# Recommendation tower on one core: ten embedding tables by one-hot matmul, taken two at a time, and features laid out by pairs of samples

## The reference

```python
e = jnp.stack([tbl_0[ids[:, 0]], ..., tbl_25[ids[:, 25]]], axis=1)
combined = jnp.concatenate([dense_features[:, None, :], sparse_features], axis=1)   # 512 x 27 x 128
interactions = jnp.einsum('bfd,bgd->bfg', combined, combined)
interactions_flat = interactions[:, iu, ju]                                         # 351 pairs
h = jnp.concatenate([dense, interactions_flat, dense], axis=1)                      # 607
h = jnp.maximum(h @ W_top1 + b_top1, 0.0)     # 512
h = jnp.maximum(h @ W_top2 + b_top2, 0.0)     # 256
y = h @ W_top3                                # 1
```

## Time and profile before

| what | us |
|---|---|
| median of 3 runs | 112.77 (111.9 to 113.47) |
| span of the profiled execution | 110.6 |
| PE busy | 98.0 (89%) |
| DVE busy | 87.3 (79%) |
| ACT busy | 85.4 (77%) |
| POOL busy | 67.7 (61%) |
| stage one on PE, first to last one-hot matmul | 7.92 to 60.3 |
| stage two on PE | 60.9 to 108.7 |

### The profile page before, as it was taken

How to read it: one execution, slowest core, us unless ns; L and a number is a source line. 1 busy time by engine, 2 the same in 40 slices (tenths; PEclk the granted TensorE clock), 3 DMA queues, 4 the chain that set the end, 5 groups by cost and what they waited for, 6 DMA issues and landing times. The chain is left out here.

```text
span 110.6 us, 2569 instructions
## 1 busy us (share of the span) xinstructions
PE 98.0 (89%) x931; PEld 77.7 (70%) x931; DVE 87.3 (79%) x216; ACT 85.4 (77%) x180; POOL 67.7 (61%) x68
## 2 busy tenths in 40 slices
PE   4967989949999999999999976999999977987991
PEld 2334846538788877768667965899899876975960
DVE  4469989689999999988989899945992849999001
ACT  4369697999999999999971899966796679683310
POOL 3577777777777777788888977777777700000000
PEclk9999999999999999999999999999999999999999
DMA  4889989944987789999110123212222210000000
GB/s 75 278 294 362 357 246 390 330 169 76 281 172 261 289 170 381 413 378 310 56 27 25 42 68 77 65 49 61 67 70 54 74 25 0 6 0 0 0 0 1
DMA packets 7868, 16.59 MB, mean 150 GB/s; under 512 B 2156, under 2 KB 3568, under 8 KB 7600
## 3 DMA queue, kind: packets, MB, share of 16 engines
q1 hardware_dynamic: 5648, 11.84, 31.9%
q0 software_dynamic: 1920, 3.94, 12.6%
q10 hardware_dynamic: 288, 0.66, 2.2%
HBM read 16.43 MB, written 0.00 MB: 148 GB/s over the span
## 5 line engine op out<-in xcount | busy, mean ns | idle before, releaser
L329 POOL DMA_INDIRECT rows<-in_gathered_tables,row_at x60 | 66.8, 1114 | 20.1 <-issue 17.7
L695 PE MATMUL gram_ps<-one_hot,table_hi 128*128 128x512 f32 x94 | 38.8, 413 | 4.3 <-DVE one_hot L512 2.5
L697 PE MATMUL gram_ps<-one_hot,table_lo 128*128 128x512 f32 x94 | 37.0, 394 | 0.0
L512 DVE TENSOR_SCALAR one_hot<-hot_ids_sb,row_ids 128x512 fp32r<-128x512 int32 x83 | 35.4, 480 | 1.9 <-DMA hot_ids_sb<-in_hot_ids 1.9
L540 DVE COPY pairs<-gram_ps 27x128 f32<-27x128 f32 (+3 forms) x76 | 25.3, 333 | 6.0 <-PE gram_ps L633 4.9
L695 PEld LDWEIGHTS gram_ps<-one_hot,table_hi 128*128 128x128 f32 x94 | 17.6, 188 | 13.3 <-DVE one_hot L512 5.4
L435 ACT COPY pairs<-gram_ps 27x128 f32<-27x128 f32 (+3 forms) x68 | 22.7, 334 | 3.9 <-PE gram_ps L633 3.1
L697 PEld LDWEIGHTS gram_ps<-one_hot,table_lo 128*128 128x128 f32 x94 | 17.7, 189 | 2.5
L633 PE MATMUL gram_ps<-features_t 128*59 128x56 f32 x512 | 15.9, 219 | 1.9 <-ACT features_t L344 1.3
L633 PEld LDWEIGHTS gram_ps<-features_t 128*59 128x59 f32 x512 | 14.7, 134 | 3.6 <-ACT features_t L344 1.7
L400 ACT COPY features_t<-gram_ps 128x512 f32<-128x512 f32 (+2 forms) x12 | 12.3, 1040 | 4.9 <-PE gram_ps L697 4.9
(11 more groups left out here) (45 smaller groups left out, 58.1 us busy)
## 6 DMA issues: line engine op xcount, KB each, us to landing
table_sb<-in_hot_tables SPq DMA_DIRECT2D x10, 512.0 KB, 5.6
hot_ids_sb<-in_hot_ids SPq DMA_DIRECT2D x11, 256.0 KB, 4.8
w_pairs_sb<-in_w_pairs SPq DMA_DIRECT2D x1, 1024.0 KB, 8.6
w_again_sb<-in_w_again SPq DMA_DIRECT2D x1, 1024.0 KB, 11.2
rows<-in_gathered_tables,row_at POOLq DMA_INDIRECT x60, 4.9
table_sb<-in_hot_tables ACTq DMA_DIRECT2D x1, 512.0 KB, 5.2
w_sb<-in_w SPq DMA_DIRECT2D x1, 512.0 KB
table_sb<-in_hot_tables SPq DMA_DIRECT2D x2, 128.0 KB, 5.3
```

The source lines that it names most:

```text
L329: pool.indirect_dma_start(rows[:, p % rows_ring, m, :], None, gathered_tables, bass.IndirectOffsetOnAxis(ap=row_at[:, t, at:at + 1], axis= ...
L512: nc.vector.tensor_scalar(one_hot_at(i), hot_ids_sb[:, of % ids_ring, :], row_id(n, c), None, ALU.is_equal).then_inc(one_hot_dve, 1)
L695: nc.tensor.matmul(hot_bank(of), table_hi[:, n % 3, own], one_hot_at(i), start=(begins and c == 0), stop=False)
L697: last = nc.tensor.matmul(hot_bank(of), table_lo[:, n % 3, own], one_hot_at(i), start=False, stop=(ends and c == count - 1))
```

## The change

- Table 0 (10 parts) is gathered, not multiplied: ten hot tables with 84 parts, sixteen gathered with 64 indirect DMAs (16 per tile; a tile's first pass has four, the others three). `rows` holds 7 passes, not 9.
- The hot tables run in groups of two (`HOT_GROUPS`; the first and last group have one table). One DVE instruction makes the one-hot rows of both tables (128x1024, L509 of the changed kernel); ACT makes none. The split in high and low goes by pieces of four parts, with two PSUM banks in turn, not three.
- `features_t` is laid out by pairs of samples: two samples' numbers for one slot are neighbours, so a copy of one table writes 8 bytes in every 256. The products' operands are read with a step of two numbers; they have 64 and 54 columns (before 59 and 56). The transposes write PSUM without a step. The samples are reordered on input, so that the copies into `pairs` write neighbouring numbers.
- The two sets of dense weights are loaded compactly (128x1024), added by one instruction, and moved to their places in `w_pairs_sb` by 14 DMAs on SP, ahead of the ten DMAs that join the dense features.
- The zeroing of `pairs` and of half of the free slots goes to POOL, ahead of the gathers. Two warm-up matmuls, not four.

```diff
-HOT = (0, 2, 3, 1, 7, 13, 16, 19, 21, 23, 25)
-HOT_PARTS = (10, 10, 10, 8, 8, 8, 8, 8, 8, 8, 8)
+HOT_GROUPS = ((1,), (2, 3), (7, 13), (16, 19), (21, 23), (25,))
+GROUP_PARTS = (8, 10, 8, 8, 8, 8)
+PIECE_PARTS = 4
...
-TURN_EARLY = {5 + p: p for p in range(9)}
-WARM = (4, 4, 4, 2)
+TURN_BEHIND = {(1, 4): 0, (1, 9): 1, (2, 3): 2, (2, 7): 3, (3, 3): 4, (3, 7): 5, (4, 3): 6, (4, 7): 7, (5, 7): 8}
+WARM = (4, 4)
...
-    table_ring, ids_ring, rows_ring = 5, 5, 9
+    piece_ring, ids_ring, rows_ring, hot_ring = 8, 3, 7, 8
...
-        features_t = sbuf("features_t", [P, batch, SLOTS])
+        features_t = sbuf("features_t", [P, batch // 2, SLOTS, 2])
...
# SP, after the loads of the weights
+                sp.wait_ge(w_summed, 1)
+                sp.wait_ge(pair_weights_in, 16)
+                for d, (p, i) in enumerate(dense_places()[:dim]):
...
+                        sp.dma_start(w_pairs_sb[p:p + run, i, :], w_dense_sb[d:d + run, 0, :]).then_inc(w_joined, 16)
+                sp.wait_ge(pairs_zeroed, 1)
                 join_dense(0)
                 join_dense(1)
...
# ACT, stage one
+                for g in range(n_groups):
+                    if g >= 1:
+                        place_hot(g - 1)
...
+                    for q in ahead[:2]:
+                        split_piece(q)
+                    for p in turns[:-1]:
+                        place_pass(p)
+                    for q in ahead[2:]:
+                        split_piece(q)
...
+                    for p in turns[-1:]:
+                        place_pass(p)
...
# DVE, stage one
+                        if 1 <= g < n_groups - 1:
+                            behind = (5, 6, 8, 9) if g == 1 else (1, 3, 5, 7)
+                            if c in behind and behind.index(c) < len(pieces_of(g + 1)):
+                                low_part(pieces_of(g + 1)[behind.index(c)])
+                        if g == n_groups - 1 and c == 3:
+                            sum_dense_weights()
...
# PE, products
-                            last = nc.tensor.matmul(gram_ps[64 * h:64 * h + SLOTS + FEATURES, n % 2, q, 0:4 * COLUMNS],
-                                                    flat_features[:, b * SLOTS:b * SLOTS + SLOTS + FEATURES],
-                                                    features_t[:, b:b + 2, 0:2 * COLUMNS], start=True, stop=True)
+                            last = nc.tensor.matmul(gram_ps[64 * h:64 * h + 2 * SLOTS, n % 2, q, 0:2 * FEATURES],
+                                                    features_t[:, two:two + 2, :, h].rearrange("p a s -> p (a s)"),
+                                                    features_t[:, two:two + 2, 0:FEATURES, h], start=True, stop=True)
...
-                pe.wait_ge(w_summed, PAIR_PARTS)
+                pe.wait_ge(w_joined, 16 * n_w_runs)
                 layer1(0, (0, 1, 2, 3))
```

More of the change, by code:

```diff
@@ L58, in pair_places @@
                     yield 32 * k + g, i, None, False
-FREE_ROWS = ((27, 5, 0, 4), (59, 5, 0, 4), (91, 5, 0, 3), (123, 3, 0, 3), (64, 64, 3, 1))
+FREE_ROWS = ((27, 5, 0, 4), (59, 5, 0, 4), (91, 5, 0, 3), (64, 64, 3, 1), (123, 5, 0, 3))
 def dense_places():
-    return [(p, i) for row, rows, part, parts in FREE_ROWS for p in range(row, row + rows) for i in range(part, part + parts)]
+    return [(p, i) for row, rows, part, parts in FREE_ROWS for i in range(part, part + parts) for p in range(row, row + rows)]
 def pieces():
@@ L76, with sample_order @@
 PIECES = pieces()
+def sample_order():
+    return [first + (2 * h + a) * (size // 4) + q for first, size in PIECES for q in range(size // 4) for a in range(2) for h in range(2)]
 def pieces_through(sample):
@@ L199, in pair_block @@
             first, size = PIECES[n]
[L200 to L204 removed]
+            nq = size // 4
+            b = first % P + nq * j
@@ new lines, in row_id, with tables_through, hot_table, parts_through @@
+        def row_id(g, c):
+            return row_ids[:, int(GROUP_PARTS[g] != GROUP_PARTS[-1]), c:c + 1]
+        def tables_through(g):
+            return sum(len(group) for group in HOT_GROUPS[:g + 1])
+        def hot_table(g, t):
+            return tables_through(g) - len(HOT_GROUPS[g]) + t
+        def parts_through(g, c):
+            return PARTS.index((g, c)) + 1
+        def piece_uses(q):
+            g, t, first, count = PIECES_HOT[q]
+            return parts_through(g, first + count - 1)
@@ new lines, in pieces_of, with piece_columns, piece_with @@
+        def pieces_of(g):
+            return [q for q, piece in enumerate(PIECES_HOT) if piece[0] == g]
+        def piece_columns(of, q, c=None):
+            g, t, first, count = PIECES_HOT[q]
+            span = slice(0, count * dim) if c is None else slice((c - first) * dim, (c - first + 1) * dim)
+            return of[:, q % piece_ring, span]
+        def piece_with(g, t, c):
+            return [q for q, (pg, pt, first, count) in enumerate(PIECES_HOT) if (pg, pt) == (g, t) and first <= c < first + count][0]
@@ new lines, in place_hot @@
+                def place_hot(g):
+                    act.wait_ge(part_used, parts_through(g, GROUP_PARTS[g] - 1))
+                    for first, end in ((0, BLOCK), (BLOCK, batch)) if g == n_groups - 1 else ((0, batch),):
+                        for t in range(len(HOT_GROUPS[g])):
+                            act.copy(features_t[:, first // 2:end // 2, 1 + hot_table(g, t), :],
+                                     hot_bank(g, t)[:, first:end].rearrange("p (b two) -> p b two", two=2)).then_inc(hot_placed, 1)
@@ L595, in turn_pass @@
                         pe.wait_ge(placed, p - 1)
[L596 to L602 removed]
+                    pe.wait_ge(rows_in[p], 16 * gathers_of(p))
+                    for m in range(gathers_of(p)):
+                        last = nc.tensor.transpose(turn_ps[:, p % 2, m * P:(m + 1) * P], rows[:, p % rows_ring, m, :], ident[:, :])
+                    last.then_inc(turned, 1)
                 def turn_last_pass():
@@ new lines, in _ @@
+                for g, c in PARTS:
+                    if c == 0 and g >= 2:
+                        pe.wait_ge(hot_placed, tables_through(g - 2))
+                    pe.wait_ge(one_hot_made, parts_through(g, c))
+                    for t in range(len(HOT_GROUPS[g])):
+                        q = piece_with(g, t, c)
+                        if c == PIECES_HOT[q][2]:
+                            pe.wait_ge(hi_made, q + 1)
+                            pe.wait_ge(lo_made, q + 1)
+                        nc.tensor.matmul(hot_bank(g, t), piece_columns(table_hi, q, c), one_hot_at(g, c)[:, t, :],
+                                         start=(c == 0), stop=False)
+                        last = nc.tensor.matmul(hot_bank(g, t), piece_columns(table_lo, q, c), one_hot_at(g, c)[:, t, :],
+                                                start=False, stop=(c == GROUP_PARTS[g] - 1))
+                    last.then_inc(part_used, 1)
+                    if (g, c) in TURN_BEHIND:
+                        turn_pass(TURN_BEHIND[g, c])
@@ L776 @@
     tables = [_np.asarray(inputs[f"tbl_{i}"]) for i in range(TABLES)]
-    ids = _np.asarray(inputs["ids"])
+    ids = _np.asarray(inputs["ids"])[order]
     single = ids[:, list(GATHERED[:SINGLE])].reshape(-1, 128, SINGLE).transpose(1, 0, 2)
```

402 lines of the change are left out of this document (158 added, 244 removed).

## The result

The changed kernel took **119.12 us** (median of 4 runs, 118.44 to 120.08) and the kernel before 112.87 us (median of 4, 111.9 to 113.47): a ratio of **1.058, interval 1.049 to 1.066**. That is 5.8% slower. The forecast's wide range of 109.3 to 119.5 holds the median with 0.4 us to spare, and one of the four executions lies above it. The forecast's own case, 114.3 us with bounds of 111 to 116.5, and its likeliest verdict, "no change", did not come about. The profiled execution took 118.44 us with a span of 116.6, against 110.6 before. Where executions of one kernel lie more than 1.5% apart, ratios are taken from the quicker ones.

The account below looks back on a forecast made before the run. The loop between PE, ACT and DVE was to decide: 110.6 us span + 1.2 stage one + 1.2 join - 0.9 copies = 112.1, plus 2.2 to the median: 114.3 us. Range 109.3 to 119.5.

Parts of the forecast that it names:

- The forecast's own case: Whole kernel: span 112.1 us, time 114.3 us, 1.4% more than before; range 111 to 116.5, chance 0.57.
- no change: Verdict on the whole kernel: time within 2% (2.3 us) of the kernel before; chance 0.42.
- placements at 0.90 us: Third rival, ACT: table placements stay at 0.90, adding 3.0 us, 117.3 us in all; chance 0.14.
- The loop: Stage one, PE, ACT and DVE: PE stalls 2.3 us in groups 2 to 4, 1.3 more in 2 and 3; ends 61.5.
- The seam: Between stage one and layer one: late joins hold DVE's fold; layer one starts at 72.3 us; 1.2 us added to span.
- A wide one-hot: DVE's 128x1024 one-hot takes 0.68 us; lower bound 0.60, upper 0.83.
- A placement of a table: ACT, runs of two numbers: 0.52 us between starts, bounds 0.52 and 0.90; by the cache-line rule, full speed.
- The copies into pairs: Writing in one run, about 1.0 ns a number, 128 numbers near 0.28 us; 0.9 us saved in all.
- by the number of columns nothing changes: PE's products with 64 and 54 columns instead of 59 and 56: no added time taken.
- The rival on the step: Second rival, PE's products: operands slow at a step of 8 bytes; span 122, time 124 us; chance 0.12.
- The gathers: POOL: the 64th gather starts near 89.2 us, lands at 92, needed about 98; covered by 6 us.
- The first rival: Loop does not bind: stage one ends at 52.0, gathers bind, span 106.6, time 108.8 us; chance 0.17.

Follow-up runs that it names:

- fills_again: Changed kernel with PE's waits filled by identity products and four identity blocks at the start, ACT's order kept; second round: 116.83 us, 1.043 of the kernel before.
- changed_again: The changed kernel itself, unedited, run again: 118.83 us, ratio 1.060 to the kernel before.
- products_in_one_run: Changed kernel with ACT splitting pieces before waiting for PE, and product operands read as contiguous runs (pairs wrong): 107.86 us, one execution.
- loop_open: Changed kernel, but from group 2 ACT splits four pieces before waiting for PE: 143.03 us in the disturbed first round, 108.34 us (0.965) in the second.
- all_together: Changed kernel with ACT splitting pieces before waiting for PE, dense weights summed one group earlier, three warm-up matmuls: 108.14 us, 0.964 of the kernel before.
- narrow_one_hots: Changed kernel with ACT splitting pieces before waiting for PE, and two one-hots of 512 replacing each of 1024: median 113.67 us, 1.001 of the kernel before.
- no_weight_dmas: Changed kernel without the 14 summed-weight transfers and PE's wait for them: 145.5 to 152.6 us in the disturbed first round; 117.83 us (1.047) in the second.

## Why the forecast held, and where it did not

The median lies in the wide range, 4.8 us above the forecast of 114.3, and that is in part luck: the upper part of the range was there for placements at 0.90 us (117.3) and for the forecast's edge, and neither is what happened. The loop was forecast in kind and nearly in size; the clock was not in the forecast at all.

**The loop** is right in its links and its places: five waits, at parts three and seven of groups 2 and 3 and at part three of group 4. Expected were 2.3 us three times and 1.3 twice; measured were 2.36, 2.34 and 2.44, and 0.77 and 0.53. Group 1 ended at 23.6 on PE, expected 23.7. But a group takes 12.35 us even at the full clock (fills_again; 12.34 in changed_again), not 11.7: the step was too short by about 0.6 us in each of three groups, shared by the two halves of a group (6.70 and 5.65 us from turn to turn, expected 6.4 and 5.3). That is 1.8 of the 3.3 us by which stage one ended late (64.8 against 61.5).

**The clock** was the step that was missing. Before, it stood at the full level throughout and I read nothing into that. In the changed kernel a stall of 2.4 us with a few matmuls behind it is followed by a stretch at 1.2 GHz in place of 2.4, in groups 2 and 3. It costs 1.7 us of stage one in the profiled execution and 2.9 in changed_again, and 2.0 of the whole by the medians. The Trainium skill (TensorE: Matmul & The Clock Gate, Part 1) says that the throttled state is the default and activity releases it; the trace agrees in part: granted were 0.94, 0.86 and 0.83 from 25 to 30, 30 to 40 and 40 to 50 us, where the stalls of groups 2 and 3 lie, but 1.00 from 50 us on, although group 4 has the longest stall of all, 2.44 us. So no run here tells which stall brings the clock down. Who forecasts waits on PE has to add what the matmuls behind them may cost.

**The seam** came out at nearly the length that I gave it, 11.3 us from the last turn against 10.8, but for another reason, so that was luck. I had the joins land late, and DVE's fold wait for them; but the fold never waited. The 14 transfers took 0.70 us each and not 0.55, and held up PE's products and the first copies, which the forecast did not have. Without them over it the seam is 8.5 us, a microsecond shorter than before (9.6). The faster copies would bring that; no run changed them alone.

**Prices.** A wide one-hot takes 0.70 from start to start (expected 0.68). A placement of a table goes every 0.50 us (0.52): here the trace shows runs of two numbers, and they agree with what the prediction took from the Trainium skill (Advanced Engine Details and Errata, Memory Cachelines); the rival at 0.90 fell. The copies into pairs took what I gave them:

```profile
L542 DVE COPY pairs<-gram_ps 27x128 f32<-27x128 f32 x28 | 8.1, 290 | 15.4 <-remote 7.5 <-PE gram_ps L633 7.5
```

290 ns where it was 388. Behind the start of layer one 0.9 us less was expected and 0.2 came, since the products, which I had at nothing, took 1.0 us more there. Two thirds of that is the other shape, by products_in_one_run, and "by the number of columns nothing changes" was wrong. The rival on the step had the right direction and the wrong size: it decides from 0.035 us a record, and a record takes 0.0334.

**The gathers** were covered, as expected; the last one started at 88.92 (89.2).

The sum: 112.1 expected for the span, 116.6 measured. Of the 4.5 us, 1.8 are the loop, 1.7 the clock (together 3.3 by the ends of stage one), 0.5 the seam and 0.7 the stretch behind layer one (40.5 where 39.8 were expected). The first rival, that the loop does not bind, is what loop_open built: it said 52.0 for the last turn, gathers that bind, and 108.8 us in all; 52.02, a chain over the gathers, and 108.34 were measured. The prediction was right to give it a low chance with this order of ACT. The run shows that everything else of the change, table 0 gathered, wide one-hots and compact weights, is together worth 3.5%, and that the order in which ACT takes its work turns it into a loss of 6%.

## What to carry to other kernels

When a change makes two helper engines cheaper, look not at their busy shares but at the order of their queues: if A's next input for B stands behind something that waits for C, and C waits for B, each takes the whole round trip in turn, and their idle shares grow. The cure here was a few lines of order, with no byte more of memory. And before counting time given back at a seam as gained, ask for which wait it will be exchanged: in all_together one wait of 2.3 us on PE, with the low clock behind it, cost a microsecond more than three gaps of 0.8 us in all and copies that started 2.3 us later.

## What the runs showed of the chip that was not expected

- Fourteen small transfers from SBUF to SBUF, issued 0.70 us apart, delayed three compute engines for as long as they were issued: 4.5 to 5.8 us from the last turn to the first copy in the five executions with them over the first products, 2.7 to 3.0 in the four without. By which way is open.
- The granted clock fell behind a wait of 2.3 to 2.4 us and some matmuls, in stage one as in all_together's stage two; 64 products of 2.14 us took 3.67 there. It did not fall behind every such wait: in the changed kernel's profile the wait of 2.44 us in group 4 left it at 1.00.
- Beside DVE's narrow one-hots in narrow_one_hots each gather on POOL took 1.88 us instead of some 1.0, in step with DVE's period of 2.18 us.
- A whole set of runs, of the kernel before too, took some 25 us more, with all engines idle together and no releaser in the trace. In it products that wait for nothing went out one by one, 0.5 to 1.9 us apart, for some 11 us:

```profile
75.49 0.21 PE L640 MATMUL gram_ps<-features_t 128*64 128x54 f32 x1 [0.45 <-issue]
...
79.07 0.25 PE L640 MATMUL gram_ps<-features_t 128*64 128x54 f32 x1 [1.83 <-issue]
```

These are rows of loop_open in the first round. They look like the seam's gaps, many times as long, but they are there in no_weight_dmas too, so the 14 transfers are not their cause. The cause stays open.
